# Self-attention's query and key weights multiplied into one matrix on the chip, one projection of the tokens in place of two

## The reference

```python
x = x + xattn(layernorm(x), ctx, ctx, Wq, Wk, Wv, Wo, bo)      # 16 heads
x = x + attn(layernorm(x), Wq, bq, Wk, bk, Wv, bv)             # below
x = x + ffn(layernorm(x), w1, b1, w2, b2)                      # gelu, signs of w1 and w2

def attn(x, Wq, bq, Wk, bk, Wv, bv):
    q = x @ Wq + bq
    k = x @ Wk + bk
    v = x @ Wv + bv
    scores = einsum('btd,bsd->bts', q, k) / sqrt(512)
    scores = where(causal, scores, -1e30)
    m = max(scores, axis=(-2, -1), keepdims=True)       # one maximum and one sum
    e = exp(scores - m)                                 # for a whole sequence
    w = e / sum(e, axis=(-2, -1), keepdims=True)
    return einsum('bts,bsd->btd', w, v)
```

## Time and profile before

| | us |
|---|---|
| median of 3 runs | 2921.3 |
| lowest and highest | 2920.09, 2921.76 |
| span of the profiled execution | 2917.1 |
| median less that span | 4.2 |
| PE busy in it | 2794.1 (96%) |
| DVE busy | 1668.3 (57%) |
| ACT busy | 1267.4 (43%) |
| POOL busy | 776.4 (27%) |

### The profile page before, as it was taken

One profiled execution on the slowest core, in us unless ns is written; L12 is line 12 of the kernel. 1 busy time (PEld: TensorE's weight loads), 2 busy tenths in 40 slices (PEclk: granted clock), 3 DMA queues, 4 the chain that ended last, 5 costly groups with the idle time before them and its releaser, 6 DMA issues. The chain is left out here.

```text
span 2917.1 us, 54809 instructions
## 1 busy us (share of the span) xinstructions
PE 2794.1 (96%) x18492; PEld 1704.0 (58%) x18492; DVE 1668.3 (57%) x3620; ACT 1267.4 (43%) x2954; POOL 776.4 (27%) x1530
## 2 busy tenths in 40 slices
PE   7999999999999999999999999957999999899999
PEld 4455555555555555555555555534666666566666
DVE  7555555555555555555555555556665666656664
ACT  4344444444444444444444444423433443344444
POOL 2233333333333333333333333211111111111110
PEclk9999999999999999999999999978999999999999
DMA  4211111111111111111111111022000000000000
GB/s 143 83 56 55 62 41 40 40 48 41 40 40 48 41 40 40 48 41 40 40 48 41 40 40 48 13 84 66 15 30 15 15 14 22 22 14 14 14 23 15
DMA packets 65959, 118.49 MB, mean 41 GB/s; under 512 B 12016, under 2 KB 32496, under 8 KB 65392
## 3 DMA queue, kind: packets, MB, share of 16 engines
q1 hardware_dynamic: 65904, 117.76, 12.4%
HBM read 109.06 MB, written 8.65 MB: 40 GB/s over the span
## 5 line engine op out<-in xcount | busy, mean ns | idle before, releaser
L656 DVE SCALAR_TENSOR_TENSOR kT_lo<-psum,kT_hi 128x512 f16<-128x512 f32 x256 | 177.1, 692 | 440.2 <-ACT kT_hi L587 440.2
L591 ACT ACTIVATE v_hi<-psum 128x512 f16<-128x512 f32 x256 | 152.8, 597 | 552.7 <-PE psum L746 552.7
L746 PE MATMUL psum<-c_hi,xWk_hi 128*128 128x512 f16 x1024 | 388.1, 379 | 2.3 <-PEq L136 2.3
L746 PE MATMUL psum<-xWv_hi,c_hi 128*128 128x512 f16 x1024 | 388.3, 379 | 0.0
L746 PE MATMUL psum<-xWv_lo,c_hi 128*128 128x512 f16 x1024 | 388.1, 379 | 0.0
L746 PE MATMUL psum<-xWv_hi,c_lo 128*128 128x512 f16 x1024 | 388.1, 379 | 0.0
L746 PE MATMUL psum<-c_lo,xWk_hi 128*128 128x512 f16 x1024 | 388.1, 379 | 0.0
L746 PE MATMUL psum<-c_hi,xWk_lo 128*128 128x512 f16 x1024 | 388.1, 379 | 0.0
L118 POOL TENSOR_TENSOR c_lo<-ctx_raw,c_hi 128x1024 f16<-128x1024 f32 x128 | 272.5, 2129 | 429.8 <-ACT c_hi L583 419.2
L662 DVE SCALAR_TENSOR_TENSOR v_lo<-psum,v_hi 128x512 f16<-128x512 f32 x256 | 177.1, 692 | 360.4 <-ACT v_hi L591 360.4
L597 ACT ACTIVATE e<-psum,neg_max 128x257 f32<-128x257 f32 x512 | 236.3, 474 | 281.9 <-DVE neg_max L651 281.9
(11 more groups left out here) (195 smaller groups left out, 5986.9 us busy)
## 6 DMA issues: line engine op xcount, KB each, us to landing
ctx_raw<-in_ctx_main SPq DMA_DIRECT2D x128, 512.0 KB, 3.3
xs<-in_x SPq DMA_DIRECT2D x8, 1024.0 KB, 5.5
v_rep<-v_last_rows SPq DMA_DIRECT2D x512, 16.0 KB, 2.3
xb<-in_x SPq DMA_DIRECT2D x16, 512.0 KB, 3.3
out<-res_out SPq DMA_DIRECT2D x32, 256.0 KB, 2.0
ffn_raw<-in_w_t SPq DMA_DIRECT2D x11, 512.0 KB, 3.4
late_raw<-in_late_w SPq DMA_DIRECT2D x4, 1024.0 KB, 4.7
res<-in_w_t SPq DMA_DIRECT2D x5, 512.0 KB, 3.5
```

Source lines behind the costliest of these rows:

```text
L591: nc.scalar.mul(v_hi[u][:, t, :], v_bank(t), W_UNSCALE).then_inc(v_hi_done, 1)
L656: nc.vector.scalar_tensor_tensor(out=kT_lo[r][:, m, :, 0:S], in0=k_bank(m), scalar=W_UNSCALE, in1=kT_hi[r][:, m, :, 0:S], op0=ALU.mult, op ...
L746: mm = nc.tensor.matmul(bank, a, b, start=(n == 0), stop=(n == len(steps) - 1))
```

## The change

The scores are (x Wq + bq)(x Wk + bk)^T. Written out, they are x (Wq Wk^T) x^T, a term that depends on the key's token alone, one that depends on the query's token alone, and a constant. The changed kernel makes M = Wk Wq^T once, projects the tokens by it (`y`), and takes the scores of `y` with the normalised tokens themselves. The vector Wk bq is added to `y` as a bias (`key_bias`), the query-token term is the product of the token with Wq bk (`row_bias`, the same in all rows), summed on DVE in `row_biases` and added to the row's maximum and to the exponent's shift.

`cross_queries` gets two more "groups", 8 and 9: `sWq` and `sWk` are loaded into `xs` in place of tokens, transposed and split by the same steps, and after `last_tokens` PE makes M (four banks of twelve matmuls), `row_bias` (twelve matmuls of 512 columns) and `key_bias` (48 matmuls of one column). `last_tokens` now stands after the last query group and these transposes. `late_hi` has three slots; `LATE` is 2, with two weights left for `cross_attention` to load. In a round of `token_stages` 48 matmuls of 256 columns are left of 96.

```diff
@@ cross_queries, SP: the two weights as groups NG and NG + 1
+            for u in range(2):
+                g = NG + u
+                sp.wait_ge(t_ps, TILES * (g - 1))
+                sp.dma_start(xs[u][:, :, :], late_w[1 + u].rearrange("p (c n) -> p c n", c=KC)
+                             ).then_inc(x_landed[u], 16)
+            for n, b in enumerate((bq, bk)):
+                sp.dma_start(bias_col[:, n, :], b).then_inc(bias_landed, 16)
             for b in range(6):
                 load_context(nc, sp, ctx_main, contexts, b, b % 4)
@@ cross_queries, ACT
-                if not more:
-                    last_tokens()
                 high_q(g, FIRST)
-                if more:
-                    high_xT(g + 1, 1 - u)
+                high_xT(g + 1, 1 - u)
                 high_q(g, LAST)
...
             groups(act, one)
+            act.wait_ge(bias_landed, 32)
+            nc.scalar.mul(bk_hi[:, :, :], bias_col[:, 1, :].unsqueeze(2).to_broadcast([P, KC, P]), W_SCALE
+                          ).then_inc(bias_hi_done, 1)
+            nc.scalar.mul(bq_hi[:, :, :], bias_col[:, 0, :].unsqueeze(2), W_SCALE).then_inc(bias_hi_done, 1)
+            high_xT(NG + 1, 1)
+            for b in range(2):
+                first_context(b)
+            last_tokens()
+            for b in range(2, 4):
+                first_context(b)
+            for m in range(KC):
+                act.wait_ge(fold_ps, m + 1)
+                nc.scalar.mul(M_hi[:, m, :], fold_bank[m], FOLD_SCALE * W_UNSCALE * W_UNSCALE
+                              ).then_inc(fold_hi_done, 1)
...
@@ cross_queries, PE
             groups(pe, one)
+            transposes(NG + 1, 1)
+            last_tokens()
+            pe.wait_ge(xT_lo_done, (NG + 2) * TILES)
+            pe.wait_ge(q_lo_done, KC * NG)
+            for m in range(KC):
+                run(fold_bank[m], [(q[:, k, m * P:(m + 1) * P], kk[:, k, :]) for k in range(KC)
+                                   for q, kk in passes(xT_hi[0], xT_lo[0], xT_hi[1], xT_lo[1])]
+                    ).then_inc(fold_ps, 1)
+            pe.wait_ge(bias_lo_done, 2)
+            run(row_bias_bank, [(b[:, k, :], q[:, k, :]) for k in range(KC)
+                                for b, q in passes(bk_hi, bk_lo, xT_hi[0], xT_lo[0])]).then_inc(row_bias_ps, 1)
+            for m in range(KC):
+                mm = run(key_bias_bank[:, m:m + 1], [(kk[:, k, m * P:(m + 1) * P], b[:, k, :])
+                                                     for k in range(KC)
+                                                     for kk, b in passes(xT_hi[1], xT_lo[1], bq_hi, bq_lo)])
+            mm.then_inc(key_bias_ps, 1)
@@ token_stages, ACT
-                    for r in range(4):
-                        eng.wait_ge(s["qk_ps"], 4 * n + r + 1)
-                        past(eng, s["qk_lo_done"], 4 * n + r - 1)
+                    for r in range(2):
+                        eng.wait_ge(s["y_ps"], 2 * n + r + 1)
+                        past(eng, s["y_lo_done"], 2 * n + r - 1)
@@ token_stages, DVE
+            def row_biases(n):
+                for t in range(T):
+                    dve.wait_ge(s["norm2_done"], T * n + t + 1)
+                    nc.vector.scalar_tensor_tensor(out=xu[:, t, :], in0=xn[:, t, :], scalar=1.0, in1=row_bias[:, :],
+                                                   op0=ALU.mult, op1=ALU.mult,
+                                                   accum_out=r_bias[:, t:t + 1]).then_inc(s["r_done"], 1)
+                dve.wait_ge(s["r_done"], (T + 1) * n + T)
+                nc.vector.tensor_scalar(r_shift[:, :], r_bias[:, :], 1.0, EXP_SHIFT, ALU.mult,
+                                        ALU.add).then_inc(s["r_done"], 1)
...
                 link(nc.vector.reduce_max(row[:, :], sc[:, :, :], AX.X), CHAIN * n + 1)
+                link(nc.vector.tensor_tensor(row_r[:, :], row[:, :], r_bias[:, :], ALU.add), CHAIN * n + 2)
...
-                F(2, 3, 4)
+                F(2)
+                if front:
+                    row_biases(n)
+                F(3, 4)
@@ token_stages, PE
-                    for r in range(4):
-                        hi, lo = late["sWq" if r < 2 else "sWk"]
+                    for r in range(2):
                         for c in range(2):
-                            m = 2 * (r % 2) + c
-                            mm = run(chunks(g_bank(QK_BANK[r]), 2)[:, c, :],
+                            m = 2 * r + c
+                            mm = run(chunks(g_bank(Y_BANK[r]), 2)[:, c, :],
```

More of the change, by code:

```diff
@@ L96, in perceiver_block @@
                           heads_hi, heads_lo, xWk_hi, xWk_lo, xWv_hi, xWv_lo, k_last_hi, k_last_lo,
-                          v_last_rows, contexts)
+                          v_last_rows, contexts, late_w, bq, bk, late_hi, late_lo, key_bias, row_bias)
             cross_attention(nc, sem_in, sb_in, psum, ctx_main, v_last_rows, xWk_hi, xWk_lo, xWv_hi,
@@ L122, in cross_queries @@
 def cross_queries(nc, sem_in, sb_in, psum, x, xWq, xWk, xWv, ctx_main, ctx_last, ident, ones, heads_hi,
-                  heads_lo, wk_hi, wk_lo, wv_hi, wv_lo, k_last_hi, k_last_lo, v_last_rows, contexts):
+                  heads_lo, wk_hi, wk_lo, wv_hi, wv_lo, k_last_hi, k_last_lo, v_last_rows, contexts, late_w,
+                  bq, bk, late_hi, late_lo, key_bias, row_bias):
     KC, TOKENS = heads_hi.shape[1], heads_hi.shape[2]
@@ L408, in _, with run @@
             pe.wait_ge(w_lo_done, 1)
+            def run(bank, steps):
+                for n, (a, b) in enumerate(steps):
+                    mm = nc.tensor.matmul(bank, a, b, start=(n == 0), stop=(n == len(steps) - 1))
+                return mm
             def one(g, u, more=True):
-                if not more:
-                    last_tokens()
                 queries(g, u, FIRST)
-                if more:
-                    transposes(g + 1, 1 - u)
+                transposes(g + 1, 1 - u)
                 queries(g, u, LAST)
             groups(pe, one)
+            transposes(NG + 1, 1)
[9 more added lines that the diff above has]
+                                for b, q in passes(bk_hi, bk_lo, xT_hi[0], xT_lo[0])]).then_inc(row_bias_ps, 1)
+            for m in range(KC):
+                mm = run(key_bias_bank[:, m:m + 1], [(kk[:, k, m * P:(m + 1) * P], b[:, k, :])
+                                                     for k in range(KC)
+                                                     for kk, b in passes(xT_hi[1], xT_lo[1], bq_hi, bq_lo)])
+            mm.then_inc(key_bias_ps, 1)
 def cross_attention(nc, sem_in, sb_in, psum, ctx_main, v_last_rows, wk_hi, wk_lo, wv_hi, wv_lo,
@@ L816, in _, with token_stages @@
                 step(QUADS - 1, u, more=u < 3, key=u < 2)
-def token_stages(nc, sem_in, sb_in, psum, x, bo, bq, bk, bv, b1, b2, w1_t, w2_t, late_hi, late_lo,
-                 ident, ones, heads_hi, heads_lo, SCALE, out):
+def token_stages(nc, sem_in, sb_in, psum, x, bo, bv, b1, b2, w1_t, w2_t, late_hi, late_lo, key_bias,
+                 row_bias, ident, ones, heads_hi, heads_lo, SCALE, out):
     TOKENS, D = x.shape
```

170 lines of the change are left out of this document (110 added, 60 removed).

## The result

| | before | after |
|---|---|---|
| median, us (4 runs each) | 2921.5 | 2842.4 |
| lowest and highest | 2920.1, 2924.3 | 2841.7, 2845.9 |
| span of the profiled execution | 2917.1 | 2841.0 |
| mean granted clock | 0.980 | 0.984 |

The ratio is 0.973, 95% interval 0.9716 to 0.9743: 79.2 us faster. I had said 2856 with a range of 2847 to 2866.

A forecast was written before the change was run, and what follows sets the result against it. PE, busy for 96% of the span, bounds the kernel. Span 2917.1 + 17.6 (`cross_queries`) - 78.6 (matmuls, rounds 1 to 15) - 4.0 (round 0) = 2852.1 us; the median stands 4.2 higher: 2856 us, range 2847 to 2866.

The forecast's parts named there:

- The wait stays: In each round PE's wait for `gelu_lo(2)` ahead of `layer2(2)`, 3.58 us, held by POOL's addition, remains unchanged.
- That stays too: In a round, PE's half clock (1.2 GHz) behind the `gelu_lo(2)` wait, from 2309.84 to before 2312.92, remains unchanged.
- Rival C: Half clock behind the wait not entered in part of the rounds: up to 20 us, time 2837 to 2850; chance 0.07.
- three signs: PE waiting for `x2T_lo` each round; first two `row_biases` instructions over 1.2 us each; over 2 us waiting between `key_bias` and `cross_attention`.
- 48 matmuls a round, 5.24 us: Projections in rounds 1 to 15: 48 of 96 matmuls removed, 5.24 us a round, 78.6 us in all, no new wait.
- Row biases hidden: On DVE behind `gelu_lo(2)`: 1.75 us of `row_biases` a round fit in 2.78 us of idle time, costing nothing.
- `cross_queries` +17.6: Folding work on PE in `cross_queries`: 19.1 us of transposes and matmuls added, barrier partly won back, net +17.6 us.
- Contexts hidden: End of `cross_queries`: delayed context loads and splits finish near 141 to 143 us, just hidden behind PE ending near 143.
- Rival A: In rounds, row biases on DVE outlast their cover: 0.2 to 0.7 us a round, time 2859 to 2867; chance 0.12.
- Rival B: End of `cross_queries` set by late contexts, or `cross_attention` begins at half clock: 2 to 7 us, 2858 to 2863; chance 0.10.
- Round 0, -4.0: Round 0: DVE 3.3 us earlier, two fewer column loads 0.9, longer maxima chain +0.2; in all -4.0, between 0 and -6.
- The 4.2 us around the span: Whole kernel: the median was taken to stand 4.2 us above the profiled span, added to the forecast span of 2852.1.

The follow-up runs named there:

- the filled kernels: 28 unread matmuls a round put ahead of PE's wait for `gelu_lo(2)`, in both kernels: 2827.7 us for the changed kernel, 2894.9 for the one before.

## Why the prediction was wrong, step by step

- **"The wait stays": right.** 3.58 us in each of rounds 1 to 14 (round 15 hasn't got it), and 56.7 us for all of PE's waits for `gelu_lo`, before and after.
- **"That stays too" (the half clock behind it): wrong, the step that failed.** After, five rounds of fourteen are at the floor, where before only round 1 was, and of the others fewer are of the costlier kind: two of nine, where before six of thirteen were. The sum left this term at nothing; it was 11.1 us by the filled kernels. Rival C named it, with 0.07, and the measured time lies in its 2837 to 2850. None of the three signs by which I wanted to know that I was wrong looked at the clock, and none of them came.
- **Its size: wrong too.** I read one round and put the half clock at 1.3 us; that round was one of the two cheapest of the thirteen (58.7 us). The mean is 27.7 / 14 = 1.98 us before and 1.19 after. The row that I took for a round of 54.4 us was a stretch cut out of one; a round is 59.3. The starts of all rounds would have shown lengths from 58.7 to 60.3 with no difference in work: a sign that something beside the work sets them.
- **48 matmuls a round, 5.24 us: right.** 14 rounds at the floor give 802.75 - 729.46 = 73.3, and 73.4 was the sum; the last stretch gives 5.2. No wait came in at the scores: the last `y_lo` is done at 2145.72 and PE comes to them at 2146.96, 1.24 us to spare, as I had it.
- **Row biases hidden: right, but by less than I read.** They take 0.68 us each with 0.08 for reading the sum, and are done at 2136.1; the two `gelu_lo` behind them end at 2136.80, and DVE begins `x2T_lo` at 2136.89. The cover of 2.78 us was that of a round at half clock, in which the transposes are late. In the one round before at full clock it was 1.52, against 1.4 for the row biases:

```profile
2016.08 1.29 DVE L1133 TENSOR_TENSOR x2T_lo<-psum,x2T_hi 128x512 f16<-128x512 f32 x2 [1.52 <-ACT x2T_hi L1072]
```

  For the instruction shape on which "Vector Engine (DVE) Microarchitecture Reference" of the Trainium skill ("Points that are easy to get wrong") has half throughput, two SBUF sources and none bf16, the trace has 679 ns: as long as the plain 684 ns, and as the 687 ns on the mean of such an instruction on two f32 sources of which one is in PSUM (`res` from `psum` and `xb`). Its rule doesn't show here; what a bf16 source would make of it no run tells. Rival A did not come.
- **`cross_queries` +17.6: 1.7 too much.** It took 15.9. The one-column matmuls cost 1.2 us instead of 2.6; the barrier gave back 1.8 instead of 1.5. The rows, to be held against the earlier trace rows:

```profile
104.51 1.91 PE L444 MATMUL psum<-ident,xs 128*128 128x128 f32 x16
...
141.02 0.17 PE L484 MATMUL psum<-bq_hi,xT_hi 128*128 128x1 f16 x1
141.05 0.16 PE L484 MATMUL psum<-bq_lo,xT_hi 128*128 128x1 f16 x1
...
142.21 0.16 PE L484 MATMUL psum<-bq_hi,xT_lo 128*128 128x1 f16 x1
142.89 0.38 PE L836 MATMUL psum<-c_hi,xWk_hi 128*128 128x512 f16 x1 [0.52 <-PEq L143]
```

  48 of them start within 1.19 us, 0.025 each. The Trainium skill's 25 ns ("TensorE: Matmul & The Clock Gate", "Back-to-back issue gap") agrees with it; its 62 ns, which is for hardware decode off, doesn't show here.
- **Contexts hidden: right.** PE's wait at the barrier is 0.5 us. Rival B is out.
- **Round 0, -4.0: it was -1.8.** Two loads fewer gave nothing: the issue of `b_col` took 2.20 us instead of 0.43, and `b_row`, for which POOL waits, let it go 7.05 us after its issue instead of 6.4.

```profile
1935.73 2.20 SPq L1095 DMA_DIRECT2D b_col<-in_b  x1
...
1938.45 0.43 SPq L1097 DMA_DIRECT2D b_row<-in_b  x1
```

```profile
1945.50 2.34 POOL L1123 TENSOR_TENSOR xb<-xb,bo_row 128x1024 f32<-128x1024 f32 x1 [10.62 <-DMA b_row<-in_b]
```

- **The 4.2 us around the span: too much.** The profiled execution of the changed kernel took 2842.8 us with a span of 2841.0, so 1.8. I had put against a median what was partly scatter between runs.

From my 2856: -11.0 for the clock in rounds 1 to 14, -1.7 for the folding, -1.4 in `cross_attention` (not followed up), +0.9 ahead of the folding, +2.2 in round 0, -2.8 around the span and between runs.

**What stays open:** what decides in which rounds the clock falls. The runs show that it falls behind 3.6 us of an idle PE in most rounds, not in all, and in none behind 0.5 us; that the same wait behind the same work gives either; and that a length 2.6 us longer has less of it and one 5.2 us longer more. That the lengths and starts of the rounds decide it fits all of this, but is argued and not shown. So no run shows that a shorter round must gain more than its matmuls, as it did here. An idle time between 0.54 and 3.58 us wasn't tried.

## What to carry to other kernels

A wait on the bounding engine had two prices here: its length, and what the clock took back behind it. The second is to be read from all rounds (their lengths, and the granted clock of each) and not from one, and a change of the rounds' work can change it with the wait untouched; a range should hold the time with all of it and with none of it. Here the wait, which I left as it was in my forecast, was worth more than half as much as the whole change and went away with one line: when the profile shows an engine held by another's traffic, try the other's start.

## What the runs showed of the hardware that I had not expected

- More work can be less time: 420 unread matmuls in PE's idle time made the kernel before 25 us faster and the changed one 15.
- After equal waits of 3.58 and 3.59 us PE went on at 2.4 GHz once (2134.76) and was at 1.2 GHz some 0.5 us behind the wait the other time (2080.99); in other rounds it came out of the wait at 1.2 GHz already (2294.50, clock 0.55 over 6.17 us).
- A DVE multiply of two f32 sources in SBUF with a sum took 679 ns for 512 columns and 76 ns for the sum; a plain addition of that size took 684 ns.
- Beside POOL's addition of 1024 columns a DVE subtraction of 256 took 2.55 us instead of 0.42, and beside POOL's copies two DVE tensor_scalar instructions took 2.42 instead of 1.00.
